# Attention scores as three 64-row products with a pair's two heads in the row halves of TensorE, in place of two stacked 128-row products per head

## What is computed

```python
q = _heads(seq_inputs @ Wq + bq)
k = _heads(seq_inputs @ Wk + bk)
v = _heads(seq_inputs @ Wv + bv)
scores = jnp.einsum('bhqd,bhkd->bhqk', q, k) / np.sqrt(HEAD_SIZE)
bias = jnp.where(graph_mask, 0.0, NEG)[:, None]
probs = jax.nn.softmax(scores + bias, axis=-1)
ctx = jnp.einsum('bhqk,bhkd->bhqd', probs, v)
ctx = ctx.transpose(0, 2, 1, 3).reshape(...)
out = _layernorm(x + ctx @ Wf + bf)
```

## Time and profile before

| | us |
|---|---|
| three timed runs | 1620.15, 1620.8, 1623.42 |
| median | 1620.8 |
| span of the profiled execution | 1678.4 |

### The profile page before, as it was taken

One profiled execution on the slowest core, in us unless ns is written; L12 is line 12 of the kernel. 1 busy time (PEld: TensorE's weight loads), 2 busy tenths in 40 slices (PEclk: granted clock), 3 DMA queues, 4 the chain that ended last, 5 costly groups with the idle time before them and its releaser, 6 DMA issues.

```text
span 1678.4 us, 30828 instructions
## 1 busy us (share of the span) xinstructions
PE 1557.5 (93%) x10320; PEld 1236.2 (74%) x10320; DVE 1111.9 (66%) x2044; ACT 896.1 (53%) x1605; POOL 345.4 (21%) x656
## 2 busy tenths in 40 slices
PE   7989989999899998999898998999989998999994
PEld 6867778677777777777686776877768676787773
DVE  6667657676667666677565775767756676577672
ACT  5556545565355544556445564466644565446561
POOL 1222022221222211222112221122211222112111
PEclk9999999999999999999999999999999999999997
DMA  4112112121122211212112121122210321112210
GB/s 135 43 43 59 32 43 70 30 45 33 43 70 36 45 27 43 70 40 53 26 31 73 34 50 32 31 73 45 45 33 24 78 47 39 34 31 36 45 32 25
DMA packets 110893, 76.47 MB, mean 46 GB/s; under 512 B 59776, under 2 KB 98432, under 8 KB 110720
## 3 DMA queue, kind: packets, MB, share of 16 engines
q1 hardware_dynamic: 110720, 74.29, 18.3%
HBM read 36.31 MB, written 12.78 MB: 29 GB/s over the span
## 4 chain that ended last, share of the span: by engine, by line
PE 41%; DMA 32%; issue 14%; SPq 5%; DVE 4%; POOL 2%; ACT 1%; POOLq 0%; DVEq 0%; ACTq 0%
DMA spread_dram<-inv_sum 24%; PE turn_ps L448 9%; PE score_ps L438 9%; PE context_ps L463 8%; DMA inv_rows<-spread_dram 5%; PE misc_ps L371 4%; PE misc_ps L373 4%; PE misc_ps L372 4%; DMA q_swap<-q_home 3%; SPq L328 3%; PE score_ps L371 1%; PE score_ps L372 1%; PE score_ps L373 1%; SPq L281 1%; DVE prob L608 1%
## 5 line engine op out<-in xcount | busy, mean ns | idle before, releaser
L608 DVE CUSTOM_DVE_ANT_0 prob<-score_ps,mask 128x1024 f32<-128x1024 f32 x384 | 468.3, 1221 | 65.1 <-PE score_ps L438 57.7
L541 ACT ACTIVATE prob<-prob,row_min 128x1024 f32<-128x1024 f32 x384 | 439.7, 1145 | 57.4 <-DVE row_min L608 52.0
L534 ACT ACTIVATE prob_t<-turn_ps 128x512 f32<-128x512 f32 x384 | 229.4, 597 | 396.4 <-PE turn_ps L448 388.9
L448 PE MATMUL turn_ps<-ident,prob 128*128 128x128 f32 x3072 | 413.9, 277 | 4.8 <-DVE prob_t L617 3.7
L463 PE MATMUL context_ps<-prob_t,v_all 128*64 128x256 f32 x3072 | 380.4, 392 | 33.3 <-DVE context L628 33.3
L448 PEld LDWEIGHTS turn_ps<-ident,prob 128*128 128x128 f32 x3072 | 343.4, 141 | 85.8 <-issue 64.3
L617 DVE COPY prob_t<-turn_ps 128x512 f32<-128x512 f32 x384 | 264.9, 690 | 180.8 <-PE turn_ps L448 177.9
L463 PEld LDWEIGHTS context_ps<-prob_t,v_all 128*64 128x64 f32 x3072 | 207.7, 139 | 179.7 <-issue 60.2
L728 POOL TENSOR_TENSOR context_lo<-context,context_hi 128x256 fp32r<-128x256 f32 x96 | 70.5, 734 | 1122.3 <-ACT context_hi L552 1122.3
L438 PE MATMUL score_ps<-k_stack,q_home 128*128 128x512 f32 x768 | 270.2, 433 | 11.6 <-DMA q_swap<-q_home 10.5
L438 PE MATMUL score_ps<-k_stack,q_swap 128*128 128x512 f32 x768 | 241.5, 396 | 0.0
(11 more groups left out here) (59 smaller groups left out, 1805.5 us busy)
## 6 DMA issues: line engine op xcount, KB each, us to landing
q_swap<-q_home SPq DMA_DIRECT2D x192, 128.0 KB
x_in<-in_x_dram SPq DMA_DIRECT2D x32, 384.0 KB, 6.0
inv_rows<-spread_dram SPq DMA_DIRECT2D x192, 64.0 KB, 3.9
out_dram<-res SPq DMA_DIRECT2D x32, 384.0 KB, 3.0
adj_in<-in_adj_dram SPq DMA_DIRECT2D x64, 128.0 KB, 3.6
spread_dram<-inv_sum SPq DMA_DIRECT2D x96, 2.0 KB
prob_t<-in_L_gnn_Wk_dram SPq DMA_DIRECT2D x1, 576.0 KB, 4.0
prob_t<-in_L_gnn_Wq_dram SPq DMA_DIRECT2D x1, 576.0 KB, 7.2
```

Of the source, the lines that this page charges most:

```text
L448: last = pe.transpose(turn_ps[:, half, i, :], prob[:, u % 3, kt * P:(kt + 1) * P], ident[:])
L534: nc.scalar.activation(prob_t[:, pair % 2, head, 0:4, qt * P:(qt + 1) * P], turn_ps[:, 0], ACT.Copy).then_inc(copied[0], 1)
L541: nc.scalar.activation(prob[:, t % 3, :], prob[:, t % 3, :], ACT.Exp, scale=-1.0, bias=row_min[:, t % 4:t % 4 + 1], accum_out=row_sum[:, t ...
L608: nc.vector.tensor_tensor_reduce(prob[:, t % 3, :], score_ps[:, t % 2, :], mask[:, qt, :], 1.0, HUGE, ALU.add, ALU.min, row_min[:, t % 4:t ...
```

## The change

`k_stack`, `q_home` and `q_swap` give way to `k_hi`, `k_lo`, `q_hi` and `q_lo`, each with 128 rows for a pair of heads: the even head in rows 0 to 63, the odd head in rows 64 to 127, just as the projection leaves them. ACT and VectorE write them in one instruction of 128 rows each. The DMAs to `q_swap`, their semaphores and SyncE's waits for them are gone. Scores of both units of a round are made at the even step: for each of the three products and each key half one matmul of 64 rows and 512 columns for each head, twelve in all. The low x low product is left out. The wait ahead of them is for the masks of both units of the round before, and for VectorE's low part of q instead of the transfers.

```diff
@@ buffers
-        k_stack = sb("k_stack", [P, HEADS, S], F32R)
-        q_home = sb("q_home", [P, HEADS, GQ], F32R)
-        q_swap = sb("q_swap", [P, HEADS, GQ], F32R)
+        k_hi = sb("k_hi", [P, 3, S], F32R)
+        k_lo = sb("k_lo", [P, 3, S], F32R)
+        q_hi = sb("q_hi", [P, 3, GQ], F32R)
+        q_lo = sb("q_lo", [P, 3, GQ], F32R)
@@ SyncE
-            def swap_q(b, job):
-
-                pair = job[1]
-                sp.wait_ge(job_out, jobs_through(b, job))
-                for to, at in ((0, 64), (64, 0)):
-                    sp.dma_start(q_swap[to:to + 64, 2 * pair:2 * pair + 2, :].bitcast(F32),
-                                 q_home[at:at + 64, 2 * pair:2 * pair + 2, :].bitcast(F32)
-                                 ).then_inc(q_swapped[pair], 16)
...
@@ TensorE
-                    if kind == "scores":
+                    if kind == "scores" and step[1] % 2 == 0:
                         t = step[1]
-                        group, pair, head, qt = t // 12, t % 12 // 4, t % 2, t % 4 // 2
-                        h = 2 * pair + head
-                        pe.wait_ge(masked, b * UNITS + (t + 1))
-                        if t < 2:
-
-                            pe.wait_ge(job_out, first_jobs_through(b, first[6 + 2 * t]))
-                        if t % 4 == 0:
-
-                            pe.wait_ge(q_swapped[pair], b * 128 + 32 * (group + 1))
+                        group, pair, qt = t // 12, t % 12 // 4, t % 4 // 2
+                        pe.wait_ge(masked, b * UNITS + (t + 2))
+                        if t == 0:
+                            pe.wait_ge(job_out, first_jobs_through(b, first[8]))
+                        if t % 4 == 0 and group:
+                            pe.wait_ge(job_out, jobs_through(b, ("q", pair, group)))
                         q = slice(qt * P, (qt + 1) * P)
-                        for n, q_stack in enumerate((q_home, q_swap)):
+                        last = [None, None]
+                        for n, (q_part, k_part) in enumerate(((q_hi, k_hi), (q_hi, k_lo), (q_lo, k_hi))):
                             for half in range(2):
                                 keys = slice(half * 512, half * 512 + 512)
-                                last = pe.matmul(score_ps[:, t % 2, keys], q_stack[:, h, q], k_stack[:, h, keys],
-                                                 start=(n == 0), stop=(n == 1))
-                        last.then_inc(scores_done, 1)
+                                for head in range(2):
+                                    rows = slice(64 * head, 64 * head + 64)
+                                    last[head] = pe.matmul(score_ps[:, head, keys], q_part[rows, pair, q],
+                                                           k_part[rows, pair, keys], start=(n == 0), stop=(n == 2))
+                        for head in range(2):
+                            last[head].then_inc(scores_done, 1)
@@ ACT
-                width, stack, cols, heads = job_parts(job)
-                for head, rows, _ in heads:
-                    last = nc.scalar.activation(stack[rows, head, cols], job_bank(b, job)[rows, 0:width], ACT.Identity,
-                                                bias=bias_qk[rows, 1 if kind == "k" else 0, n:n + 1])
-                last.then_inc(hi_done, 1)
+                width, hi, _ = job_parts(job)
+                at = 1 if kind == "k" else 0
+                nc.scalar.activation(hi, job_bank(b, job)[:, 0:width], ACT.Identity,
+                                     bias=bias_qk[:, at, n:n + 1]).then_inc(hi_done, 1)
@@ VectorE
-                width, stack, cols, heads = job_parts(job)
-                for head, rows, other in heads:
-                    last = nc.vector.scalar_tensor_tensor(
-                        out=stack[other, head, cols], in0=job_bank(b, job)[rows, 0:width],
-                        scalar=bias_qk[rows, 1 if kind == "k" else 0, n:n + 1], in1=stack[rows, head, cols],
-                        op0=ALU.add, op1=ALU.subtract)
-                last.then_inc(job_out, 1)
+                width, hi, lo = job_parts(job)
+                at = 1 if kind == "k" else 0
+                nc.vector.scalar_tensor_tensor(out=lo, in0=job_bank(b, job)[:, 0:width], scalar=bias_qk[:, at, n:n + 1],
+                                               in1=hi, op0=ALU.add, op1=ALU.subtract).then_inc(job_out, 1)
```

More of the change, by code:

```diff
@@ L210, in graph_attention @@
         job_out = sem("job_out")
-        q_swapped = [sem(f"q_swapped{pair}") for pair in range(3)]
         projected = sem("projected")
@@ L256, in job_parts @@
             if kind == "k":
[L257 to L261, removed]
+                cols = slice(piece * 512, piece * 512 + 512)
+                return 512, k_hi[:, pair, cols], k_lo[:, pair, cols]
+            return GQ, q_hi[:, pair, :], q_lo[:, pair, :]
         def vector_normalises(group, with_next):
@@ L313, in body @@
                     kind = step[0]
-                    if kind == "job" and step[1][0] == "q":
-                        swap_q(b, step[1])
-                    elif kind == "denominators":
+                    if kind == "denominators":
                         pair = step[1]
@@ L346, in body @@
                                      res[:, 2 * group:2 * group + 2, :]).then_inc(stored[group], 16)
-            for pair in range(2):
-                swap_q(None, ("q", pair, 0))
             sp.wait_ge(mask_done, 2)
@@ L353, in _ @@
                              adj_rows[GQ + qt * P:GQ + (qt + 1) * P, :]).then_inc(adj_loaded[qt], 16)
-            swap_q(None, ("q", 2, 0))
             with sp.Fori(0, BATCH - 1) as b:
```

## The result

Four timed runs gave 1642.5 us in the median (1633.0 to 1643.7) against 1620.5 for the kernel before beside them: a ratio of 1.0143, 95% interval [1.0097, 1.0189], so slower. Two later comparisons, on chips where the kernel before takes 1664 to 1670 us, gave 0.9994 [0.9957, 1.0031] and 0.9985 [0.9951, 1.0019]: no difference. The forecast was faster by 49 us; no comparison shows a gain. That 1642.5 us lie in the stated range of 1505 to 1660 says nothing for the forecast, since that range also holds the kernel before.

A forecast was written before the change was run, and what follows sets the result against it. TensorE's own stream was taken to bound the kernel. Score block -40, transfers -10.5, writes -14 and round trip +16 gave -48.5 us, so 1572 us after carrying over the profiled-to-timed difference; the stated range was 1505 to 1660.

The forecast's parts named there:

- What bounds the kernel: TensorE's own stream sets about 13.2 of 13.9 us per pair of rounds, 5.63 us a round without jobs; the rest is waits.
- The trip: Denominators' way through DRAM and back, ahead of `context`: gives back 0.4 us at 40 of 96 pairs, 16 us (bounds 0 and 30).
- Score matmuls: TensorE's score block: the two heads' matmuls overlap, so twelve cost six starts of 0.23 us, 1.38 us, against 1.86 before.
- change of mode: Array switches around each score block: 0.27 us a round, making the block 1.65 us and saving 40 us over 192 rounds.
- The rival of the loads: Weight loads not hidden in their own row half: steps of 0.33 us, +75 us, 1672 us in all; chance 0.08.
- Pairing of scores: TensorE waiting for both units' masks before scores: costs nothing, with some 0.6 us left in a round without a job.
- High and low parts: Full-height writes of q and k on ACT and VectorE: 14 us saved, at batch starts only (bounds 0 and 20).
- The q_swap transfers: DMAs of q issued on SyncE: removing them saves the 10.5 us that scores waited for them.
- The sum: All terms together: -40 - 10.5 - 14 + 16 = -48.5 us against the profiled 1678.4 us, hence 1630, or 1572 us timed.
- the other engines eat it: Rival: VectorE's holds and the paired wait bind in most rounds, losing TensorE's 40 us; 1597 to 1640 us, chance 0.12.
- The slow end: Slow bound of the forecast, about 1597 us: loads bind, 31 us saved, no gain at batch starts, 16 given back.

The follow-up runs named there:

- `unit_by_unit`: The changed kernel with each unit's six 64-row matmuls at its own step, so the pairing is gone: 1885.7 us, 1.1333 of the kernel before.
- `split_writes`: The changed kernel with high and low parts of q and k again written in two 64-row instructions each: 1699.2 us, 1.0224 of the kernel before.
- `before_again`: The kernel before, unedited, profiled and timed again on another chip: 1665.2 us.
- `paired`: The kernel before with both units' scores issued at the even step, after both masks; layout, transfers and 128-row products stay: 1706.7 us, 1.0258 of the kernel before.
- the pair without the trip: Both kernels without the denominators' DMAs to and from DRAM, a constant standing in: 1563.0 us for the kernel before, 1567.7 us for the changed one.
- its own best list: The kernel before with the reciprocals and their DRAM write one step earlier in the list of steps: 1652.0 us, 0.9889 of the kernel before.

## Why the prediction was wrong, step by step

**What bounds the kernel.** Right in its main part: a round of TensorE's stream was put at 5.63 us and is 5.62. The list of waits was read short: beside the 33.3 and 10.5 us it has the 39.5 us for `context_lo` at batch ends, shown above, which are the round trip as well. The trip was taken for a bound that takes 16 us more after the change; it costs 100 us in either kernel, and 4 us more of TensorE's wait before mix steps (29.1 to 32.8, one trace of each) were given back.

**Score matmuls.** Side by side: right, with the price of a step right (1.58 us for the block). It was my estimate: no row of the kernel before shows row halves, and the nearest, the mix with its two heads in column halves, takes 1.88 / 16 = 0.1175 us for 256 columns, where a full-width transpose takes 0.87 / 8 = 0.109 for 128; that hinted at it and did not show it. The first step that failed is the sum around it, *change of mode*: 0.27 us were taken from the mix step's edges, which with the six steps made 1.65 us. The block's own duration of 1.58 us covers that, but two things come on top. The first matmul behind the block holds off the second (0.23 us in place of 0.12), and the kernel before had a score block start right behind the transposes: in the earlier trace rows a block adds 0.93 us, while its twin in the changed kernel starts 0.20 us after the start of the last transpose (the middle value of 175 such places in the first trace), where transposes come every 0.11. A saving of 0.21 us a round was really 0.06 to 0.10 (0.07 to 0.12 by the medians): 12 to 19 us, not 40. So each edge of the block costs some 0.1 us (0.23 - 0.12 and 0.20 - 0.11); what happens in the array there was not shown. The rival of the loads counts 0.21 us for a matmul of 512 columns by itself, and no run shows that figure: such matmuls start 0.23 us apart, in `unit_by_unit` with the loads of the same half beside them.

**Pairing of scores: cost nothing.** This is the step that took the gain away: measured alone, on the kernel before, it costs 42 us. The working went wrong at "in a round without a job". Of a batch's 24 rounds 21 have one, and VectorE's part of it stands between the two masks. The chain of the changed kernel (first comparison) runs through it from the projection to the scores:

```profile
503.22 0.57 DVE res L618
...
504.74 0.86 DVE var_eps L627
...
505.73 0.09 DVE prob_t L598
...
506.34 0.87 DVE prob L589
...
507.62 1.66 PE score_ps L422 x10
```

From 503.22 to 505.73 us VectorE works on the projection; then come the copy and the second mask, and the scores wait for the mask. Counting a job as slack for TensorE only, and not as work for VectorE, was the error. The other half of it was not seen at all: with no scores at odd steps, x jobs in neighbouring steps lie only eight transposes apart, and TensorE waits for the part before (14.5 us).

**High and low parts.** The term was mis-sized the other way: 14 us forecast, some 38 measured when they are split again. It is the same mechanism: with paired scores VectorE's work for a job stands in the loop, so taking half of it away counts behind nearly every q job (the blocks that are late in `split_writes` and not in the changed kernel) and not at batch starts alone.

**The q_swap transfers.** 10.5 us forecast; 5.5 were waited for in `before_again`, and putting them back costs some 5 us or nothing.

**The sum.** The forecast had -40 (block) - 10.5 (transfers) - 14 (writes) + 16 (trip) = -48.5, and nothing for the pairing. Three of the runs lead from one kernel to the other in steps. From the kernel before to `paired` (pairing alone) it is +42 us. From `paired` to `split_writes` (row halves and no transfers) it is 1.0258 to 1.0224, -6 us, with some 10 us of doubt from the two intervals. From `split_writes` to the changed kernel (full-height writes) it is -38 us. The end is no difference (0.9994 and 0.9985, each with 6 us of doubt). The two terms that the forecast had as small, pairing and writes, are the large ones, and they nearly cancel; the term that it had as the largest is in the noise of the full kernels, and only the pair without the trip shows it as 12 to 19 us of stream. The rival *the other engines eat it* named the mechanism, with an end of 1640 us, and was given 0.12.

**The range and the base.** The profiled execution of the kernel before was not like its timed runs. I carried its difference over to 1620.8 us. The later runs of this kernel lie between 1651 and 1685 us, and the profiled 1678.4 lie among them: the timed 1620 us were the odd ones. Its time thus differs by 3% from one comparison to another, by the chip or by something else that was not shown, while a difference of 3% was forecast from one trace. The slow end's own terms (31 saved, 10.5, 16 given back) give 1595 us, not 1597.

## What to carry to other kernels

Where work of two units is fused so that one engine produces both at once, write out the loop of the engine that consumes them with every instruction that stands between its two turns, jobs included; a margin that holds in the emptiest round says nothing of the others. After such a fusion reorder the lists: here the same change was worth nothing in the old order and 2% with two edits of the list, early reciprocals and jobs moved to where the consumer idles (1% against the kernel before with its own best list). And when measuring what a small matmul saves, compare whole rounds from start to start, since here some 0.1 us at each edge of the score block stood in its neighbours' time.

## What the hardware showed that I had not expected

- Twelve 64-row matmuls in two row halves take as long as six in one half, 1.58 and 1.59 us: side by side costs nothing at all.
- The first 128-row matmul behind a block of 64-row ones delays the next by 0.11 us (509.20, 509.43, 509.54).
- The write of 128 x 4 numbers to DRAM and its reading back cost this kernel 100 of 1665 us, by an estimate a third of it through TensorE's clock: the mean granted clock is 0.977 with them and 0.996 without. Without them six runs agree within 3 us; with them the 12 to 29 runs of an unedited kernel in one comparison scatter by 19 to 33.
